# Attention and graph convolution over 64 graphs: the degree vector made and sent first in a step, and VectorE's work behind the softmax scores in another order

## What is computed

```python
# layer 0: attention, weighted by the adjacency matrix
h = relu(layernorm(x))
q, k, v = h @ Wq.T + bq, h @ Wk.T + bk, h @ Wv.T + bv
p = adj * exp(q @ k.T)                      # 256 x 256 a graph
x1 = x + (p / p.sum(axis=2, keepdims=True)) @ v
# layer 1: graph convolution
A = adj + I
dn = A.sum(axis=-1) ** -0.5
L = A * dn[:, None] * dn[None, :]
out = x1 + L @ (relu(layernorm(x1)) @ W + b)
```

## Time and profile before

| | |
|---|---|
| median of 3 runs | 1766.1 us (1765.91 to 1770.2) |
| the profiled execution's own time | 1768.8 us |
| its span, first to last instruction | 1767.0 us |
| TensorE matmuls busy | 1720.3 us, 97% of the span |
| VectorE busy | 1294.5 us, 73% |
| ScalarE busy | 733.8 us, 42% |
| GpSimd busy | 551.4 us, 31% |
| 16 DMA engines, mean busy share of queue 1 | 41.1% |

### The profile page before, as it was taken

How to read it: one execution, slowest core, us unless ns; L and a number is a source line. 1 busy time by engine, 2 the same in 40 slices (tenths; PEclk the granted TensorE clock), 3 DMA queues, 4 the chain that set the end, 5 groups by cost and what they waited for, 6 DMA issues and landing times.

```text
span 1767.0 us, 32784 instructions
## 1 busy us (share of the span) xinstructions
PE 1720.3 (97%) x11324; PEld 1560.7 (88%) x11324; DVE 1294.5 (73%) x3097; ACT 733.8 (42%) x1546; POOL 551.4 (31%) x585
## 2 busy tenths in 40 slices
PE   7799999999999999999999999999999999999997
PEld 5799999888889999999999989989998899989996
DVE  5677777777777777777777777767777777777774
ACT  3344444443443533443443433534434344435332
POOL 1323323233233233233233233232332332332331
PEclk9899999999999999999999999999999999999998
DMA  6344345343343542443543453433434433434420
GB/s 154 50 60 72 62 59 72 54 66 70 48 73 61 59 73 61 59 73 61 59 73 60 59 73 61 59 69 46 74 72 48 73 72 48 73 62 57 74 55 27
DMA packets 218603, 114.02 MB, mean 65 GB/s; under 512 B 158944, under 2 KB 183520, under 8 KB 218592
## 3 DMA queue, kind: packets, MB, share of 16 engines
q1 hardware_dynamic: 216672, 112.30, 41.1%
q10 hardware_dynamic: 1920, 1.58, 0.3%
HBM read 80.22 MB, written 33.62 MB: 64 GB/s over the span
## 4 chain that ended last, share of the span: by engine, by line
DMA 38%; POOL 20%; PE 18%; DVE 12%; issue 11%; SPq 1%; ACT 1%; POOLq 0%; ACTq 0%; DVEq 0%
DMA dn_scratch<-dn 25%; DMA dn_row<-dn_scratch 12%; POOL xb L250 8%; PE ps L561 5%; PE ps L563 5%; PE ps L562 5%; DVE w_in L410 4%; POOL hat_hi L238 4%; POOL hat L239 4%; DVE w_in L515 3%; DVE p L524 2%; POOL dn L263 2%; DVE p_lo L530 2%; POOL hat_lo L241 2%; PE ps L571 1%
## 5 line engine op out<-in xcount | busy, mean ns | idle before, releaser
L302 ACT ACTIVATE late<-late,nb,sc 128x512 f32<-128x512 f32 x128 | 103.6, 809 | 523.0 <-DVE nb L458 523.0
L561 PE MATMUL ps<-ht_hi,m_hi 128*128 128x256 f32 x1024 | 287.4, 281 | 0.8 <-DVE wvt_lo L400 0.8
L562 PE MATMUL ps<-ht_lo,m_hi 128*128 128x256 f32 x1024 | 287.9, 281 | 0.0
L238 POOL TENSOR_TENSOR hat_hi<-adjt,eye 128x512 fp32r<-128x512 f32 x64 | 82.8, 1294 | 656.1 <-DVE p_lo L530 656.1
L563 PE MATMUL ps<-ht_hi,m_lo 128*128 128x256 f32 x1024 | 287.4, 281 | 0.0
L561 PE MATMUL ps<-w_hi,z_hi 128*128 128x512 f32 x512 | 208.5, 407 | 1.5 <-DVE z_lo L501 1.5
L563 PE MATMUL ps<-w_hi,z_lo 128*128 128x512 f32 x512 | 203.2, 397 | 0.0
L562 PE MATMUL ps<-w_lo,z_hi 128*128 128x512 f32 x512 | 203.0, 396 | 0.0
L563 PE MATMUL ps<-wvt_hi,ht_lo 128*128 128x512 f32 x512 | 202.2, 395 | 0.0
L561 PE MATMUL ps<-wvt_hi,ht_hi 128*128 128x512 f32 x512 | 202.2, 395 | 0.0
L562 PE MATMUL ps<-wvt_lo,ht_hi 128*128 128x512 f32 x512 | 202.1, 395 | 0.0
(11 more groups left out here) (100 smaller groups left out, 4523.3 us busy)
## 6 DMA issues: line engine op xcount, KB each, us to landing
x_in<-in_x_dram SPq DMA_DIRECT2D x64, 512.0 KB, 3.5
out_dram<-late SPq DMA_DIRECT2D x128, 256.0 KB, 2.1
adj_in<-in_adj_dram SPq DMA_DIRECT2D x64, 256.0 KB, 2.8
adj_blocks<-in_adj_dram SPq DMA_DIRECT2D x256, 64.0 KB
dn_row<-dn_scratch SPq DMA_DIRECT2D x64, 128.0 KB, 4.1
late<-in_L_gnn_Wk_w_dram SPq DMA_DIRECT2D x4, 256.0 KB, 4.7
late<-in_L_gnn_Wq_w_dram ACTq DMA_DIRECT2D x4, 256.0 KB, 7.6
wv_in<-in_L_gnn_Wv_w_dram SPq DMA_DIRECT2D x1, 1024.0 KB, 8.1
```

What stands on the lines that cost most here:

```text
L238: pool.tensor_tensor(hat_hi[:], adjt[:], eye[:], ALU.add).then_inc(hat_hi_ready, 1)
L302: act.activation(h1[:, t, :], x1[:, t, :], ACT.Relu, scale=sc_1[:, t:t + 1], bias=nb_1[:, t:t + 1])
L561: pe.matmul(dst, a_hi[:, c, cols], b_hi[:, c, :], start=(c == 0), stop=False)
L562: pe.matmul(dst, a_hi[:, c, cols], b_lo[:, c, :], start=False, stop=False)
```

## The change

GpSimd makes `dn` at the start of its step, before the `hat` matrices. SyncE's queue sends `dn` first and reads it back as second transfer; the loads `adj_in`, `x_in` and `adj_blocks` come behind. Since `dn` of the next graph is now made while `dn` of this one is still wanted, VectorE keeps it in `dn_kept`, and `d` is made of `dn_kept` by a multiplication with ones where it was a copy of `dn`. On VectorE `p` comes directly behind `x1b`, then `ht_lo`, `p_lo`, `s_sum`, `sd`, `dn_kept`, the score bias. ScalarE does `ht_hi` before `p_hi`.

```diff
 # SyncE, step
-                if main and ahead:
-                    sp.wait_ge(rsum_ready, this)
-                    sp.dma_start(adj_in[:], adj_next...).then_inc(adj_loaded, 16)
-                if main and ahead:
-                    sp.wait_ge(h_ready[1], this)
-                    sp.wait_ge(xb_ready, this)
-                    sp.dma_start(x_in[:], x_next...).then_inc(x_loaded, 16)
                 if main:
                     if prev:
                         sp.wait_ge(dn_row_loaded, (this - 1) * 16)
                     sp.wait_ge(dn_ready, this)
                     sp.dma_start(dn_dram..., dn[:], ...).then_inc(dn_stored, 16)
-                if main and ahead:
-                    sp.wait_ge(adjt_ready, this)
-                    load_blocks(sp, adj_next)
                 if main:
                     sp.wait_ge(dn_stored, this * 16)
                     if prev:
                         sp.wait_ge(s_sum_ready, this - 1)
                     sp.dma_start(dn_row[:], dn_dram.partition_broadcast(P)).then_inc(dn_row_loaded, 16)
+                if main and ahead:
+                    sp.wait_ge(rsum_ready, this)
+                    sp.dma_start(adj_in[:], adj_next...).then_inc(adj_loaded, 16)
+                    sp.wait_ge(h_ready[1], this)
+                    sp.wait_ge(xb_ready, this)
+                    sp.dma_start(x_in[:], x_next...).then_inc(x_loaded, 16)
+                    sp.wait_ge(adjt_ready, this)
+                    load_blocks(sp, adj_next)
 # GpSimd, step: at its start, no longer behind rs_1
+                if main:
+                    if prev:
+                        pool.wait_ge(dn_kept_ready, this - 1)
+                        pool.wait_ge(dn_stored, (this - 1) * 16)
+                    pool.wait_ge(rsum_ready, this)
+                    pool.tensor_tensor(rsum1[:], rsum[:], ones[:, 0:NT], ALU.add).then_inc(rsum1_ready, 1)
+                    pool.wait_ge(rsum1_ready, this)
+                    pool.tensor_tensor(dn[:], rsum1[:], minus_half[:], ALU.pow).then_inc(dn_ready, 1)
 # VectorE, prev
-                    dve.wait_ge(dn_ready, this - 1)
+                    dve.wait_ge(dn_kept_ready, this - 1)
                     dve.wait_ge(bn_1_done, this - 1)
-                    dve.tensor_copy(d[:], dn[:]).then_inc(d_ready, 1)
+                    dve.tensor_tensor(d[:], dn_kept[:], ones[:, 0:NT], ALU.mult).then_inc(d_ready, 1)
 # VectorE, main: new behind sd
+                    if prev:
+                        dve.wait_ge(d_ready, this - 1)
+                    dve.tensor_tensor(dn_kept[:], dn[:], ones[:, 0:NT], ALU.mult).then_inc(dn_kept_ready, 1)
```

More of the change, by code:

```diff
@@ L98, in gnn_program @@
         rsum, rsum1 = sb("rsum", [P, NT]), sb("rsum1", [P, NT])
-        dn, d = sb("dn", [P, NT]), sb("d", [P, NT])
+        dn, dn_kept, d = sb("dn", [P, NT]), sb("dn_kept", [P, NT]), sb("d", [P, NT])
         rinv = sb("rinv", [P, NT])
@@ L202, in step @@
                 if main and ahead:
-                    sp.wait_ge(adjt_ready, this)
-                    load_blocks(sp, adj_next)
+                    adj_next = adj_flat[bass.ds(sp.snap(this * (N * N)), N * N)]
+                    x_next = x_flat[bass.ds(sp.snap(this * (N * D)), N * D)]
                 if main:
@@ L254, in step @@
                     pool.tensor_tensor(rs_1[:], ve_1[:], minus_half[:], ALU.pow).then_inc(rs_1_done, 1)
[L255 to L263, removed]
                 if ahead:
@@ L335, in step @@
                                        bias=vk[:, t:t + 1]).then_inc(e_ready[t], 1)
-                    for t in range(NT):
-                        act.wait_ge(p_ready[t], this)
-                        act.activation(p_hi[:, t, :], p[:, t, :], ACT.Copy).then_inc(p_hi_ready[t], 1)
                 if ahead:
@@ L343, in step @@
                                        ps[:, HT + j, :], ACT.Copy).then_inc(ht_hi_ready[j], 1)
+                if main:
+                    for t in range(NT):
+                        act.wait_ge(p_ready[t], this)
+                        act.activation(p_hi[:, t, :], p[:, t, :], ACT.Copy).then_inc(p_hi_ready[t], 1)
+                if ahead:
                     if not main:
@@ L509, in step @@
                 if main:
+                    dve.wait_ge(adjt_ready, this)
+                    for t in range(NT):
+                        dve.wait_ge(e_ready[t], this)
+                        dve.tensor_tensor(p[:, t, :], e[:, t, :], adjt[:, t, :], ALU.mult).then_inc(p_ready[t], 1)
+                if ahead:
+                    for j in range(2):
+                        dve.wait_ge(ht_hi_ready[j], this + 1)
+                        dve.tensor_tensor(ht_lo[:, 2 * j:2 * j + 2, :].rearrange("p c n -> p (c n)"),
+                                          ps[:, HT + j, :],
+                                          ht_hi[:, 2 * j:2 * j + 2, :].rearrange("p c n -> p (c n)").bitcast(fp32),
+                                          ALU.subtract).then_inc(ht_lo_ready[j], 1)
+                if main:
+                    for t in range(NT):
+                        dve.wait_ge(p_hi_ready[t], this)
+                        dve.tensor_tensor(p_lo[:, t, :], p[:, t, :], p_hi[:, t, :].bitcast(fp32),
+                                          ALU.subtract).then_inc(p_lo_ready[t], 1)
+                if main:
                     dve.wait_ge(dn_row_loaded, this * 16)
```

23 lines of the change are left out of this document (3 added, 20 removed).

## The result

The changed kernel takes **2240.2 us** (median of 4 runs, 2236.44 to 2244.77) where the kernel before takes 1766.83 (4 runs, 1765.91 to 1770.2): 1.268 times as long, with an interval of 1.265 to 1.271. The forecast was 2002 with a range of 1840 to 2095. The sign, the place and the ring of waits that sets the pace are the forecast's; the price of one link of that ring is not, and the time lies 145 us outside the range. The profiled execution took 2244.77, with a span of 2242.9.

What follows compares the result with a forecast made beforehand. TensorE's matmuls bound the kernel before, at 26.34 us a graph; SyncE's queue would now set 29.7 plus 0.85 for the clock, taken as 30.5. 63 graphs give 1921.5, plus 3 and 78.55: about 2002 us, range 1840 to 2095.

Steps and rivals of the forecast that it cites:

- the ring of waits that sets the pace: From one `z_lo` to the next through `y`, SyncE's queue and `x_in`: 29.7 us a graph against TensorE's 26.34.
- The queue decides: SyncE's queue: three loads put behind a 9.8 us wait for the `dn` store set the pace; 79 in 100.
- The term of `x_in`'s landing: SyncE's load of `x_in`, from issue to landing: 3.5 us of the sum for a graph.
- The store, 9.8 us: SyncE's queue, from issue of the `dn` store to issue of `dn_row`: 9.8 us, taken as slow of itself.
- The first rival: `dn` store fast with nothing behind it: 23 us around, TensorE stays the bound, 1739 us; 12 in 100.
- the second rival: Store fast, GpSimd's work becomes the bound: 0.5 us a graph over TensorE's work, 1770 us; 3 in 100.
- The clock: TensorE at half clock after its wait delays the second `y`: 1.7 us a fall, every second graph, 0.85 us.
- The first member of the ring: From `z_lo` to the end of `y`: 9.0 us, and 0.85 for TensorE's half clock.
- The lower end: A store of 8.1 us and no fall of TensorE's clock: 28.0 us a graph, about 1842 us.
- VectorE's order: VectorE: `p_lo` starts 1.5 us sooner, which ends the `p_lo` waits, at most 19.4 us.
- `d` as a multiplication: VectorE: gains up to 0.8 us a graph over the copy, or nothing if held while GpSimd makes `xb`.
- GpSimd's chain: GpSimd: `hat_hi` starts at 8.1 us after `z_lo` instead of 7.0, `rs` at 14.5 instead of 13.9.

Runs made afterwards that it cites:

- experiments 1, 4 and 6: Changed kernel: 1, old queue order, 1786.11 us; 4, no store 1763.21, 8-byte pieces 1769.93, pieces 64 bytes apart 1763.63; 6, 8-byte store with matching reader, 1771.09.
- the last attempt: Changed kernel with the store of 8-byte pieces and matching reader, and `rs` moved ahead of `xb` on GpSimd: 1806.12 us, 1.034 of the kernel before.
- experiment 6: `dn` stored in 8-byte pieces, `s_sum` reading in matching order: kernel before 1737.75 us, changed kernel 1771.09 us.

## Why the forecast was right in kind and wrong in size

- **The queue decides: right.** Undoing its order takes away all but 2.3% of 26%. The ring has the forecast's six members and no other.
- **The term of `x_in`'s landing: the step that failed.** The forecast said "`x_in` to landing: 3.5 us", a row taken where `x_in` was issued ahead of the store and of `dn_row`, and 3.3 us behind `adj_in`. In the changed kernel it is issued 1.2 us behind `dn_row` and 0.6 behind `adj_in` and takes 8.1: 4.6 us more a graph, 289 us of 63 graphs. The runs split it in part. With `dn_row` from another place in DRAM `x_in` takes 5.2 to 5.4 us where the unaltered kernel takes 7.7, so 2.3 to 2.5 us are the read of `dn_scratch`. With a fast store besides it takes 3.7; but there `adj_in` is also 2.9 us ahead instead of 0.6, so whether these last 1.5 to 1.7 us are an effect of the slow store or of `adj_in` close ahead stays open. The forecast itself said that the store "holds what is behind it" and then costed the loads behind it at the price they have alone.
- **The store, 9.8 us: right that it is slow of itself, 1.3 us too long.** 8.5 us with no blocks behind it. 63 times -1.3 is -81 us. The first rival, a fast store, has fallen for this form of store. With one of 8-byte pieces (3.1 us) the queue does get out of the way, and what comes then is the second rival. The figure of some 2 us in the Trainium skill (DMA: Bandwidth & Descriptors, Anatomy of one DMA) is given there for transfers issued by GpSimd, and this store is issued by SyncE. It is near for the store 64 bytes apart, 1.6 us; for packed 4-byte pieces the trace shows 7.8 to 8.5 and decides.
- **The clock: right mechanism, undersized.** The forecast took a fall in every second graph, 0.85 us; it fell in all of them, for 1.2 us (10.05 against 8.89 with useless matmuls) in the first result and 1.8 in the later run of the changed kernel. The first member of the ring took 10.05 for the 9.85 forecast, since the 9.0 were 0.1 high (8.89 in the ring of the kernel with useless matmuls). That is 13 us.
- **The sum of these.** 4.59 - 1.29 + 0.20 + 0.22 - 0.08 = 3.64 us a graph, 229 us of the 240 by which the forecast's span was short (238 in the medians). Of the rest, 3 us are the forecast's rounding of 30.55 to 30.5, 7 us that the graphs behind the first have a mean of 34.30 where the 20 graphs have 34.19, and 1 us is the first graph, 38.15 us, for which 3 us more had been allowed.
- **The range** was made of the store and the clock, the terms seen as uncertain. The landing had a measured row and was given no end at all; a third end, `x_in` behind a held queue, would have been in the same rows. The lower end also leaves out the 3 us of the first graph: 28.0 us a graph gives 1845 and not 1842, which changes nothing here.
- **VectorE's order: the forecast's gain is real and its cost was missed.** The waits for `p_lo` went as said. But alone this order costs 4.5%, by the port that VectorE and GpSimd share; the forecast weighed that rule at `d` only. In the changed kernel the place of `dn` on GpSimd hides it.
- **`d` as a multiplication: held in part.** It takes 0.53 and 0.73 us in the graphs shown. Its median of the changed kernel is 352 ns, with 1130 the longest, where the copy had 954; the forecast's test, over 0.5 in the median, came out the other way for the changed kernel, while single ones are held as the copy was. In the variants of the changed kernel whose queue no longer sets the pace (experiments 1, 4 and 6, but for the last attempt) its median is 0.72 to 0.74 us: there it meets `xb` and is held.
- **GpSimd's chain: about as large as said.** 26.7 us a graph once the queue is out of the way, 0.4 over TensorE's 26.34 where 0.5 was named, but by the chain alone and not by a held `d` besides, as far as the waits show (experiment 6); with the fast store the changed kernel is 1771.09 - 1737.75 = 33 us behind the kernel before with the same store.

What stays open: why neighbouring 4-byte pieces are slow to store; why reading `dn_scratch` at once is slower than reading other data; how much of `x_in`'s landing is due to `adj_in` close ahead of it; and a proof by an edit that GpSimd's chain makes the 0.4 us, since the one edit that tried it moved the collision.

## What to carry to other kernels

Before moving a wait on a queue ahead of loads, take the price of those loads from a row in which they stand behind the same transfer, or treat it as unknown and give it an end in the range: the price of a transfer that runs alone says nothing of one that is queued behind a slow one. Look at how a small store lies in memory before building the order of a queue around it; here another layout of the kilobyte, with the reader changed to match it (3 to 4 us instead of 8.5 to 9.8), was worth more than the reordering. And when VectorE's operations are moved, look at what GpSimd does at the new place: two-number operations grew from 0.16 to 1.2 us there.

## What the runs showed that was not expected

- A store of 1 KB in 4-byte pieces side by side is done 7.8 to 8.5 us after its issue, in 8-byte pieces 3.0 to 3.9, in 4-byte pieces 64 bytes apart 1.6. In the kernel before, with block loads behind it, it was 9.8.
- A read of that buffer right after the store takes 6.1 us (5.8 in the later run); of other memory at the same place in the queue 3.5 to 3.9.
- Loads that no semaphore ties to the slow store are held by it as well: 8.2 us for `x_in` behind it, 3.5 ahead of it, 3.6 with no store at all.
- Filling TensorE's wait of some 6 us a graph with useless matmuls gave 108 us back, all of it in the link from `z_lo` to `y`, whose matmuls stood at half clock behind the wait.
- The hold between VectorE and GpSimd reached an operation with one SBUF input, `ve`, 1.06 us for two numbers, and slowed GpSimd's `hat_lo` from 1.29 to 1.76.
